# A two-block selective-scan and expert kernel: products with zeros in 44 units, and a new order of the work behind the logits

## The reference

```python
x = x + mamba(cond_linear(x, cond))          # both directions, DI = 512 channels, 16 states
z = cond2_linear(x, cond)                    # weights mixed by cond, plus bias
logits = z @ Wg + bg                         # 8 experts
w, top2 = softmax(top_k(logits, 2)), indices
x = x + z + sum over the two experts of (silu(zw @ W1) * (zw @ W3)) @ W2    # zw = z * w, H = 1024
```

## Time and profile before

| | us |
|---|---|
| median of 3 runs | 1397.23 |
| lowest, highest | 1395.92, 1397.71 |
| the profiled execution | 1394.14 |
| its span, first to last instruction | 1392.3 |
| PE busy, share of the span | 1294.3, 93% |
| DVE busy | 940.7, 68% |
| POOL busy | 964.5, 69% |
| ACT busy | 723.1, 52% |
| mean granted TensorE clock | 0.978 |

### The profile page before, as it was taken

How to read it: one execution, slowest core, us unless ns; L and a number is a source line. 1 busy time by engine, 2 the same in 40 slices (tenths; PEclk the granted TensorE clock), 3 DMA queues, 4 the chain that set the end, 5 groups by cost and what they waited for, 6 DMA issues and landing times. The chain is left out here.

```text
span 1392.3 us, 16616 instructions
## 1 busy us (share of the span) xinstructions
PE 1294.3 (93%) x5296; PEld 778.4 (56%) x5296; DVE 940.7 (68%) x1140; ACT 723.1 (52%) x1296; POOL 964.5 (69%) x511
## 2 busy tenths in 40 slices
PE   8999989999999989899797878899999999999997
PEld 3443333344333333333343333457999999999996
DVE  3999999999999999999999999963111111111110
ACT  4888776778785677676767564413111111111111
POOL 1999999999999999999999999832222222222211
PEclk9999999999999999999999999999999999999999
DMA  5555465555556464555456554508988888888982
GB/s 209 181 167 176 160 166 166 166 167 173 173 171 181 149 184 153 165 168 176 159 181 186 185 174 146 189 8 310 351 312 315 319 316 324 301 323 316 324 306 46
DMA packets 105497, 290.40 MB, mean 209 GB/s; under 512 B 9649, under 2 KB 19506, under 8 KB 89922
## 3 DMA queue, kind: packets, MB, share of 16 engines
q1 hardware_dynamic: 95762, 271.24, 56.3%
q0 software_dynamic: 9648, 18.09, 6.5%
HBM read 271.47 MB, written 9.96 MB: 202 GB/s over the span
## 5 line engine op out<-in xcount | busy, mean ns | idle before, releaser
L451 PE MATMUL ps_y<-arena,ident 128*128 128x512 f32 x1020 | 497.3, 619 | 55.0 <-POOL arena L1204 54.7
L1204 POOL TENSOR_TENSOR arena<-arena 128x1024 f32<-128x1024 f32 x192 | 457.4, 2404 | 18.9 <-DVE arena L946 15.3
L451 PEld LDWEIGHTS ps_y<-arena,ident 128*128 128x128 f32 x1020 | 190.9, 195 | 322.9 <-issue 214.0
L1188 POOL TENSOR_TENSOR arena<-arena 128x1024 f32<-128x1024 f32 x127 | 303.9, 2393 | 6.0 <-issue 4.3
L737 ACT ACTIVATE ps_de<-arena,An 128x512 f32<-128x512 f32 x256 | 176.2, 688 | 225.2 <-DVE arena L943 224.3
L1257 POOL DMA_INDIRECT out_x<-arena x39 | 61.8, 1584 | 319.1 <-ACT arena L881 301.9
L927 DVE TENSOR_TENSOR ps_u<-ps_du,arena 128x512 f32<-128x512 f32 x256 | 178.6, 698 | 23.9 <-DVE arena L957 8.6
L1155 DVE TENSOR_TENSOR arena<-ps_du,arena 128x512 f32<-128x512 f32 x39 | 27.0, 691 | 232.8 <-PE ps_du L617 232.8
L737 ACT ACTIVATE arena<-arena,An 128x512 f32<-128x512 f32 x256 | 181.0, 707 | 0.0
L943 DVE TENSOR_TENSOR_SCAN arena<-ps_de,hlast,arena 128x512 f32<-128x512 f32 x128 | 163.0, 1274 | 1.0 <-ACT arena L737 1.0
L943 DVE TENSOR_TENSOR_SCAN arena<-ps_de,arena 128x512 f32<-128x512 f32 x128 | 155.3, 1214 | 3.7 <-ACT arena L737 3.7
(11 more groups left out here) (225 smaller groups left out, 1484.2 us busy)
## 6 DMA issues: line engine op xcount, KB each, us to landing
arena<-bc_scratch SPq DMA_DIRECT2D x256, 512.0 KB, 4.6
arena<-in_W SPq DMA_DIRECT2D x117, 1024.0 KB, 8.2
arena<-arena POOLq DMA_DIRECT2D x15, 512.0 KB, 5.0
arena<-in_xT SPq DMA_DIRECT2D x2, 1024.0 KB, 6.1
arena<-in_w2c SPq DMA_DIRECT2D x1, 2048.0 KB, 8.6
arena<-in_xT SPq DMA_DIRECT2D x4, 512.0 KB, 6.1
X_scratch<-stg SPq DMA_DIRECT2D x12, 128.0 KB, 4.8
out_x<-stg SPq DMA_DIRECT2D x12, 128.0 KB, 5.1
```

The source lines that it names most:

```text
L451: t = e.matmul(Y[j][:, :], ident[:, :], hc[:, i % NP, j, :], start=False, stop=(n == 15))
L1188: e.tensor_tensor(uA[:, turn % 2, :, :], duA.rearrange("p (o t) -> p o t", o=1).to_broadcast([128, 2, TH]), ring[:, turn % NR, 0, :, :], A ...
L1204: e.tensor_tensor(hc[:, i % NP, :, :], hh[:, i % NH, :, :], c, ALU.mult).then_inc(gp_hc, 1)
```

## The change

Six edits:

1. In the 44 steps of `IDLE_AT` (loop steps without side work), TensorE multiplies a 128x128 block of zeros (`zeros`, cleared by POOL at the start) by 512 columns of `opT` and adds that to `Y[1]`, ahead of the wait for the unit's products. The value of the sum doesn't change.
2. The transposed products of line 557 go through channel half 0 first: the first two need only the first output block.
3. The first last tile (`last_x2(0)`) is computed ahead of the two prefix sums, where two warm-up products stood.
4. Four warm-up products, not six, stand behind the permutation product.
5. POOL's four adds of the last tiles come behind the first three fetches, and SP's four stores to the output behind the loads of the second expert's weights.
6. `lx` has memory of its own, so DVE's first products of the experts no longer wait for the stores.

```diff
--- before.py
+++ after.py
@@ -69,6 +69,12 @@
 TILE_AT = {at(2, 49): (0, 4), at(2, 53): (0, 5), at(2, 62): (0, 6), at(3, 2): (0, 7),
            at(3, 11): (0, 0), at(3, 15): (0, 1), at(3, 19): (0, 2), at(3, 23): (0, 3),
            at(3, 46): (1, 4), at(3, 50): (1, 5), at(3, 54): (1, 6), at(3, 58): (1, 7)}
+
+BUSY_AT = {i + k for at_ in (STEP_AT, CONV_AT, XD_AT, OUT_AT) for i in at_ for k in range(2)}
+BUSY_AT |= {i for at_ in (X1_AT, IN_AT, GATE_AT, LATE_AT) for i in at_} | {i + k for i in TILE_AT for k in (0, 4)}
+LIGHT_AT = {i + k for i in STEP_AT for k in range(2)}
+IDLE_AT = [i for i in range(4, NU - 4) if i not in BUSY_AT and i - 2 not in TILE_AT and
+           (i - 1 not in BUSY_AT or i - 1 in LIGHT_AT)]
 TILES = list(TILE_AT.values()) + [(1, i) for i in range(4)]
 TILE_NO = {x: k for k, x in enumerate(TILES)}
 
@@ -153,6 +159,7 @@
         mx = sb("mx", [128, NTT, E])
         mi = sb("mi", [128, NTT, E], U32)
         warmed = sb("warmed", [128, 1])
+        zeros = sb("zeros", [128, 128])
         ones_r, bias2, bgr = rows[:, 0:128], rows[:, 128:128 + C], rows[:, 128 + C:128 + C + E]
         rv = Arena(wmT[:, :, :, :].rearrange("p b k o -> p (b k o)"))
         iot, triu, ones, lane, tile_no, ids, dump, first_not = (
@@ -168,7 +175,6 @@
         xsT = af.view(2, 2, 128)
         sg = af.view(2, 512)
         hT = af.view(2, 8, 128)
-        lx = hT.rearrange("p a k t -> p (a k t)").rearrange("p (i c) -> p i c", i=4)
         yo = af.view(3, C)
         oh, pt = af.view(2, NTT, E), af.view(2, NTT, E)
         mm, cs, pa = (af.view(E, NTT) for _ in range(3))
@@ -182,6 +188,7 @@
         eid, tok, dest = (af.view(NT).bitcast(I32) for _ in range(3))
         hot, hit, rhs = af.view(NA, 128), af.view(NA, NT), af.view(NA, 2, NT)
         inv, tokf, desf = af.view(2, NT), af.view(NT), af.view(NT)
+        lx = af.view(4, 2 * C)
 
 
         l_w0, l_x0, l_ip, l_w, l_w2c, l_x, l_rc = (sem("l_" + n) for n in ("w0", "x0", "ip", "w", "w2c", "x", "rc"))
@@ -439,6 +446,9 @@
                     if n == 5 + j and q % 2:
                         e.wait_ge(ac_ev, nth_sum(q - 1, 1 - th, m))
                         e.matmul(Y[j][:, :], ident[:, :], ya[:, m, cols_of(q, th)], start=False, stop=False)
+                if i + LAG in IDLE_AT:
+                    e.matmul(Y[1][:, :], zeros[:, :], opT[:, 0:2, :].rearrange("p k o -> p (k o)"), start=False,
+                             stop=False)
                 e.wait_ge(gp_hc, i + 1)
                 if i == NU - 1:
                     e.matmul(Y[1][:, :], ident[:, :], hc[:, i % NP, 1, :], start=False, stop=True).then_inc(pe_last, 1)
@@ -480,6 +490,7 @@
             for g in range(E):
                 second_weight(1, g)
             e.wait_ge(l_late, WL)
+            e.wait_ge(gp_pad, 1)
             early_turns.extend(turns)
             taken[:] = [0] * 8
             for p in range(2):
@@ -548,15 +559,15 @@
             for h2 in range(2):
                 for c in range(2):
                     take(("xT2", h2, c), [2 * h2 + 2 + c])
-            for k in range(2):
-                is_free(("o", 1, 0, k))
             for h2 in range(2):
-                for c in range(2):
-                    p = place["xT2", h2, c][0]
-                    for k in range(2):
+                for k in range(2):
+                    is_free(("o", 1, 0, k))
+                    for c in range(2):
+                        p = place["xT2", h2, c][0]
                         t = e.matmul(PS[p][:, 0:C], wbot[:, 1, k, c * 128:c * 128 + 128],
                                      X[1][:, k, h2 * C:h2 * C + C], start=(k == 0), stop=(k == 1))
-                    t.then_inc(full[p], 1)
+                        if k == 1:
+                            t.then_inc(full[p], 1)
 
             def warm(n, p=7, w=2):
 
@@ -572,14 +583,14 @@
                     is_free(("xT2", i // 2, c))
                     e.matmul(PS[p][:, 0:E], sTt[c][:, i * 128:i * 128 + 128], wg[:, c, :], start=(c == 0), stop=False)
                 e.matmul(PS[p][:, 0:E], ones_r, bgr, start=False, stop=True).then_inc(full[p], 1)
-            warm(2, 2)
-
+
+            last_x2(0)
             mf = mm.rearrange("p e a -> p (e a)")
             e.wait_ge(dv_rt, RT["mm"])
             e.wait_ge(l_rc, 16)
             e.matmul(PS[1][:, 0:128], ones, mf, start=True, stop=True).then_inc(pe_rx, 1)
             e.matmul(PS[0][:, 0:128], triu, mf, start=True, stop=True).then_inc(pe_rx, 1)
-            for i in range(4):
+            for i in range(1, 4):
                 last_x2(i)
             for p in range(8):
                 e.wait_ge(freed[p], turns[p])
@@ -591,7 +602,7 @@
                 t = e.matmul(PS[4][:, 0:2 * NT], hot[:, c, :], rhs[:, c, :, :].rearrange("p w i -> p (w i)"),
                              start=(c == 0), stop=(c == NA - 1))
             t.then_inc(pe_inv, 1)
-            warm(6, 5)
+            warm(4, 5)
 
             def tx(i):
                 e.wait_ge(dv_xw, i + 1)
@@ -1148,10 +1159,6 @@
                 e.wait_ge(ac_sg, 2 * i + c + 1)
                 if i >= 2:
                     e.wait_ge(pe_yy, i - 1)
-                elif c == 0:
-                    for k in (2 * i, 2 * i + 1):
-                        e.wait_ge(l_lx[k], 16)
-                        e.wait_ge(l_st[2 + k], 16)
                 e.tensor_tensor(hT[:, i % 2, 4 * c:4 * c + 4, :].rearrange("p k t -> p (k t)"), PS[2 + c][:, :],
                                 sg[:, c, :], ALU.mult).then_inc(dv_hm, 1)
 
@@ -1205,6 +1212,7 @@
 
             e.memset(xp[:, 0, PAD:PAD + C], 0.0).then_inc(gp_dz, 1)
             e.memset(xp[:, :, 0:PAD], 0.0)
+            e.memset(zeros[:, :], 0.0)
             e.memset(xp[:, :, PAD + T:], 0.0).then_inc(gp_pad, 1)
             e.wait_ge(l_w, W1)
             e.tensor_tensor(dgw, ident[:, :].rearrange("p (o f) -> p o f", o=1).to_broadcast([128, NB * E, 128]),
@@ -1235,10 +1243,6 @@
                                 ALU.add).then_inc(gp_ei, 1)
             e.wait_ge(gp_ei, 3)
             e.tensor_copy(eid[:, :], cmpt[:, :, 1]).then_inc(gp_ei, 1)
-            for i in range(4):
-                is_read(e, ("x2", 1, i))
-                x2, xt = lx[:, i, 0:C], lx[:, i, C:2 * C]
-                e.tensor_tensor(xt, xt, x2, ALU.add).then_inc(gp_sB, 1)
             e.wait_ge(dv_rt, RT["tok"])
             for k in range(2):
                 e.wait_ge(l_st[k], 32 * 6)
@@ -1259,6 +1263,10 @@
 
             for i in range(3):
                 fetch(i)
+            for i in range(4):
+                is_read(e, ("x2", 1, i))
+                x2, xt = lx[:, i, 0:C], lx[:, i, C:2 * C]
+                e.tensor_tensor(xt, xt, x2, ALU.add).then_inc(gp_sB, 1)
             for k in range(4):
                 e.wait_ge(l_st[2 + k], 16)
             e.wait_ge(dv_rt, RT["des"])
@@ -1362,12 +1370,12 @@
                 is_read(e, ("x2", 1, i))
                 e.dma_start(X_dram[T + i * 128:T + i * 128 + 128, :], lx[:, i, 0:C]).then_inc(l_lx[i], 16)
             load_2(0, at_0)
+            e.wait_ge(l_xi[0], 16)
+            load_13(1, at_1)
+            load_2(1, at_1)
             for i in range(4):
                 e.wait_ge(gp_sB, i + 1)
                 e.dma_start(out[T + i * 128:T + i * 128 + 128, :], lx[:, i, C:2 * C]).then_inc(l_st[2 + i], 16)
-            e.wait_ge(l_xi[0], 16)
-            load_13(1, at_1)
-            load_2(1, at_1)
             load_13(2, at_2)
             load_2(2, at_2)
             for i in range(NW, NT):
```

## The result

The change takes **1406.16 us** (median of 7 runs, 1404.52 to 1412.1); before, run beside it 7 times, takes 1397.23 us. The ratio is **1.0067, with a 95% interval of 1.0051 to 1.0084**: slower by 9 us. The forecast was 1395.4 us with 1399.7 as its upper end, so it was wrong, and the sign was the rival's with the late sums. The changed kernel's times fall into two groups, 1404.5 to 1406.2 us (granted clock 0.973 to 0.975) and 1410.8 to 1412.1 us (0.969). The profiled execution, 1410.8 us, is one of the upper group.

The account below looks back on a forecast made before the run. DVE and POOL were taken to bound the scan's second half, TensorE the experts. Behind the scan -2.7 us, scan +0.9, sum -1.8: 1392.3 for the profiled execution, 1395.4 us from the median; range 1391.3 to 1399.7.

Parts of the forecast that it names:

- The 44 products, +0.9: Scan: products with zeros lengthen waits for sums at two places, +1.7 us; with clock gain -0.8, the scan nets +0.9.
- Clock, -0.8: Scan near 583 us: a product shortens TensorE's idle stretch, saving half of DVE's 1.53 us wait, -0.8 us.
- The tile ahead of the prefix sums, 0, ends -1.4 and +0.4: Behind the scan: a tile replaces two warm-up products; low clock stays, 0 us; from 0.4 later to 1.4 earlier.
- Channel half 0 first, -0.9: Behind the scan: two of eight products with `wbot` fill the 0.88 us wait for the second addition, -0.9 us.
- POOL's adds away, -1.9: Behind the scan: DVE's masks, conversion and two wide steps quicken without POOL's adds beside them, -1.9 us; upper end 2.2.
- The permutation product 2.8 earlier: Behind the scan: earlier masks and weight copies let this product start at 943.4 instead of 946.22 us, -2.8 us.
- the experts 3.5 earlier: Start of the experts: fetch 2.2 us earlier, 0.6 lost to stores, plus 1.3 from four warm-up products instead of six.
- The second expert's weights, +0.8: Second expert: weights come 2.2 us earlier but TensorE 3.5 earlier, a wait of up to 1.2 us; taken as +0.8.
- Sums come late: Scan rival: added products delay sums at six places, 6.9 us, no clock gained; 1401.4 us, chance 0.10; decides from 5.5 us.
- Zeros don't count: Scan rival: products with zeros do nothing for the clock, only their cost stays; 1396.2 us, chance 0.10.
- the stores queue: Experts, tile 3: output stores wait behind the second expert's weights, delaying POOL's fourth fetch, +3 us; 1400.3 us, chance 0.04.
- The signs: Right: quick masks, second-expert wait, fewer scan clock falls, DVE wait over 2 us near 227; wrong: scan's end moved over 2 us.

Follow-up runs that it names:

- kernel 4: The kernel before plus only the 27 of the 44 products with zeros that stand away from openings of new sums; ratio 0.9996 (0.9982 to 1.001).
- kernel 5: The kernel before plus only the 17 of the 44 products with zeros that stand near openings of new sums; ratio 1.0016 (1.0003 to 1.003).
- kernel 1: The kernel before plus all 44 products with zeros and nothing else; ratio 1.0049 (1.0033 to 1.0066).
- kernel 7: The kernel before plus two products with zeros at each of the 44 steps, 88 in all; ratio 1.0034 (1.0021 to 1.0048).
- kernel 9: The whole change run once more, unaltered, against the kernel before; ratio 1.0068 (1.0055 to 1.0081), median 1406.62 us.
- kernel 10: The change with the two warm-up products back ahead of the prefix sums in place of the tile, against the kernel before; ratio 1.0044, 1402.8 us.
- kernel 3: The change without products with zeros and with the two warm-up products back ahead of the prefix sums, against the kernel before; ratio 0.9993, median 1396.53 us.
- kernel 2: The change without the products with zeros, all other edits kept, against the kernel before; ratio 1.0003 (0.999 to 1.0015), median 1397.68 us.
- kernel 11: The change with the two warm-up products back ahead of the prefix sums and only the 27 products away from openings, against before; ratio 0.9989 (0.9979 to 1.0).
- kernel 6: The kernel before plus 39 products with zeros, five steps ahead of places that fell behind left out; ratio 1.0002 (0.9986 to 1.0019).

## Why the prediction was wrong, point by point

- *The 44 products, +0.9.* **This is the step that failed.** The step is the price "what they add to a wait for a sum", read from the waits that DVE already had. They cost 7 to 8 us. The price of each (0.86, 1.7 at low clock) was right, and units 224 to 227 did fall behind by 0.8, with DVE waiting 2.04 us there. Three things were missing. I took two places and an upper bound of +5.2 from the waits of DVE that the trace before already showed; the new waits stand where before had none, such as the 0.86 us at unit 56, 22 us behind the product that makes it. I counted only the sums: logits and tiles queue behind the product as well, and DVE's in-order search waits for them. And I let the product at 583 shorten a fall, where the fall grew from 6.8 to 13.7 us; the length scatters there in kernels with and without the product, so neither that growth nor a gain is shown to be its doing. How the 7 to 8 us divide over the places stays open in part, since kernels 4 and 5 don't add up to kernel 1.
- *Clock, -0.8.* With zeros alone the mean clock of the runs does rise (0.980 in kernel 4, 0.979 in 5, 0.988 in 7, for 0.976 before). In the change it doesn't: its trace has twelve low stretches in the scan where before's has eleven (58 us in all for 51), and the mean of its seven runs is 0.972. No gain came where I had put it.
- *The tile ahead of the prefix sums, 0, ends -1.4 and +0.4.* Mis-sized. In the profiled executions of the change and of kernel 9 it cost 5 to 6 us; by the medians of kernels 9 and 10, 3.8; between kernels 3 and 2, nothing that can be told. My lower and upper ends looked only at the prefix sum; at low clock the three tiles behind it, the warm-up and the permutation product (8.10 for 7.27) stretch too. The Trainium skill ("TensorE: Matmul & The Clock Gate", Part 4), cited for it, says that a transpose isn't counted as busy as a product is; the 20.5 us at 1.2 GHz in which four tiles follow each other agree with that, the 3.4 of kernel 2 do not.
- *Channel half 0 first, -0.9.* Right: scan's end to the logits 10.82 to 9.98 us.
- *POOL's adds away, -1.9.* Right, and to the upper end: the masks 4.63 us (5.15 before), the two wide steps 1.46 and 1.46 (2.02 and 1.86), the conversion 0.18 (0.68); that is 0.52 + 0.56 + 0.40 + 0.50 = 2.0 us. All six traces with the adds moved show these times; in each of the eight with the adds in their old place at least three of the four steps are slow (in kernels 4 and 5 the first wide step takes 1.46, and the masks 5.68).
- *The permutation product 2.8 earlier; the experts 3.5 earlier.* The first is right in kernel 2 (2.8); the experts start only 2.7 us earlier there. The stores did become the last wait in kernel 2, and cost 1.3 us rather than 0.6; in the other kernels with these edits they did not. From the fetch to the experts kernels 2 and 3 take 4.2 us, kernels 9 to 11 4.9, before 5.4: the four warm-up products gave 0.5 to 1.2 (forecast 1.3).
- *The second expert's weights, +0.8.* A wait is there: 1.5 us in the change, 1.6 in kernel 2, 1.2 in kernel 3, 0.5 to 0.7 in kernels 9 to 11. But kernel 1, which has none of these edits, shows 1.85. Kernel 4, which has none either, takes as long from the first expert's products to TensorE's last (424.5 us) as kernel 2 (424.6); before's 423.1 is the shortest of all traces, so the gain of the middle is in part lost against a lucky trace, and no gain behind the scan can be told in the medians.
- *The rivals.* "Sums come late" had the sign, the place and much of the mechanism, at 1401.4 us; I gave it 0.10 because DVE waited 3.2 us in all. That was the wrong evidence: a total of waits tells what is late already, and nothing of how little is early. (Its sum is 3.4 + 3.4 = 6.8, not 6.9, and 5.5 us are four fifths of it.) "Zeros don't count" and "the stores queue" didn't come.
- *The signs.* Of those named for a right forecast, the quick masks (1.16 us each), the wait before the second expert and DVE's wait over 2 us near unit 227 came; fewer falls in the scan did not. The one named for a wrong forecast came: the scan's end moved by 11.8 us.

## What to carry to other kernels

A product put into an in-order queue to fill idle time delays all that stands behind it: before placing it, read how early each result behind it is, logits and tiles too, not how long its users wait now. Put fillers only behind waits that end late anyway and away from the openings of new sums: 44 products everywhere cost 0.49%, the 27 of them placed so made no difference, and even then they brought nothing. Where the engine has no idle time left, the delay is passed on: here it came out 22 us later. Where warm-up products stand in a stretch of low clock ahead of small work, they may be what ends it; replacing them by useful but thin work saved their 3.2 us and cost up to 5 or 6 in two of three traces. And before you read a cost from one trace, look at a second trace of the same kernel: one place moved by 4.9 us between two of the change.

## What the runs showed of the hardware

A low stretch of the granted clock can last very differently long over the same instructions: 3.4 or 13.7 us from 587 us on in two traces of the same kernel, 3.4 or 20.5 us behind the logits, with busy TensorE all along (19.72 of 20.50 us in kernel 9). More products raised the mean clock as far as 0.988, but kernel 6, with five fewer than kernel 1, had 0.981 against 0.978. DVE's two wide steps took a fifth to over a quarter less time once POOL's additions were out of their time (1.46 for 2.02 and 1.86 us).
